# A pre-norm decoder layer on one core: self-attention's side work cut into smaller pieces, cross-attention's bulk loads issued behind the queries' store, the first tiles' list computed in pieces

## The chip, the cores and the metric

The kernel runs on one core of one Trainium2 chip. The metric is the device time of the program in microseconds. The engines are TensorE (PE, with its weight loads as PEld), VectorE (DVE), ScalarE (ACT), GpSimd (POOL) and SyncE (SP), which here only issues DMAs.

## What is computed

One decoder layer on x of 16 batch rows of 256 tokens with 256 features, in float32. Cut to what matters:

```python
x = x + self_attn(layernorm(x))     # 16 heads of 16; local windows of 128, and 128 global tokens
x = x + cross_attn(layernorm(x))    # 16 heads over 120 context tokens, masked
x = x + experts(layernorm(x))       # 8 experts, the top 2 of each token

# self_attn: x gets positions; w = windows of 128
local = softmax(w w^T * scale) w
comp = conv1d(x, conv_w, stride 4) + conv_b          # 64 compressed tokens
gt = concat(comp, global_memory)                     # 128 global tokens
glob = softmax(x gt^T * scale) gt
mix = sigmoid(concat(local, glob) @ gate_w + gate_b)
out = (mix * local + (1 - mix) * glob) @ out_w + out_b
```

## The kernel before

The program has two blocks, `self_attention` and `cross_and_experts`. In each, every engine has its own program, written out by hand: each engine executes its instructions in order and waits on semaphores, and nothing else orders the work.

**Self-attention.** The loop `for b in range(NB + 1)` runs over the 16 batch rows ("rows" below). A row has 8 units, and `unit(s)` splits their number into the half of the tokens, the kind (0 local, 1 global) and the half of the heads. For a unit of kind 0 TensorE makes the scores in `m.scores[0]` (`scores`, L529), VectorE takes the maxima (`maxima`, L969), TensorE subtracts them (`subtract_max`, L576), ScalarE takes exponentials (`exponentials`, L822), and TensorE multiplies by the values (`values`, L596). For a unit of kind 1 scores are made once with the queries as stationary operand for the maxima alone (`queries_scores`, L544, in `m.turn`), the maxima are transposed (`turn_max`, L557) and copied below the queries (`copy_max`, L827), and the scores are made again, already shifted, in `m.scores[1]` (`keys_scores`, L566). After every second unit VectorE transposes the output (`turn_out`, L975) and divides it (`divide`, L979 to L985), which counts up `att_read`.

Beside that stands the row's side work, which belongs to other rows: the normalised rows and their transposes for the rows ahead (`normalise` L941, `apply_norm` L952, `turn_w` L489), the context's transposes, keys and values (`turn_c`, `keys_values` L627 and L630) of the next row, the compression by convolution of the next pair of rows (`compress`, L497, in even rows only, with `add_conv_bias` L960 and `turn_g` L513), and the gate and the projection of the row before (`gate` L604, `squash` L835, `mix_row` L993 and L995, `project` L612, `residual` L1002). Gate, compression, projection and several transposes share one PSUM bank, `m.misc`; `keys_values` and one `turn_w` use halves of `m.turn`, which the units of kind 1 use too. The loop's body has four slots of two units each. Per row TensorE's side work stands so: slot 1 `turn_c` and `turn_w` or `turn_g`; slot 2 a second `turn_w` (even rows) and `keys_values`; slot 3 the whole `gate`, and in even rows the whole `compress` at its end; slot 4 `project`.

GpSimd splits the transposed rows into three bfloat16 parts (`split_w`, `split_g`, `split_k`). SyncE stores them and loads them back in stacked form, six DMAs at a time (`stack_w`, `stack_g`, helper line L228), for the next pair of rows: the queries and keys are read by `scores(b, 0)` and the global tokens by `queries_scores(b, 1)` of that pair's first row.

**Cross-attention.** The loop runs over the same 16 rows with 4 units each. Queries of row b+2 are made in row b (`queries` L1491), split on GpSimd (`split_row` L1433 to L1437), stored by SyncE to `q_scr` (`store_q` L1268) and loaded back stacked in the next turn of SyncE's loop (`stack_q`, L1262). In row b SyncE issues: the two halves of `stack_q(b+1)`, `stack_k` (even rows), the stores of x and of the normalised row b-2, `load_mask(b+3)`, `load_w2(b)`, twice some routing loads or stores, `load_v(b+2)`, and last `store_q(b+2)`. Its waits stand in that order too: `store_q` waits for GpSimd's split, and all later DMAs wait behind it. GpSimd also scatters routing entries into a table in HBM (`dispatch`, L1380).

**Experts.** Tokens are sorted into 71 tiles of 128. The first tiles need only rows 0 to 7 and their list is made by VectorE in cross-attention: `early_tiles` (with `tiles_of_experts`) at the end of row 12, `early_sources` (with `name_experts`) at the end of row 13. These are chains of operations on 8 or fewer columns, each of which waits for the one before (`step`). The tiles' outputs are added to HBM rows by accumulating stores from GpSimd (L1420).

## Time and profile before

| | us |
|---|---|
| median of 3 runs | 1221.88 |
| lowest and highest of them | 1214.57 and 1253.28 |
| profiled execution, time | 1203.42 |
| its span, first to last instruction | 1201.5 |
| TensorE busy in it | 1069.2 (89%) |
| VectorE, ScalarE, GpSimd busy | 661.3, 526.4, 553.3 |
| granted TensorE clock, mean | 0.969 |

The profile is of one execution, which is shorter than each of the three timed runs. Busy times of engines overlap; an engine's busy time beside the length of a stretch says how much of that stretch it stood idle. The four stages stand one behind the other: a start of 45 us, self-attention to about 491 us, cross-attention to about 780 us, and the experts to the end. A float32 matmul is recorded as two passes, so 8 products are 16 matmuls. In TensorE's rows a matmul's end includes the time in which its last columns drain, so consecutive groups overlap a little.

### The profile page before, as it was taken

The page shows a single profiled execution, that of the slowest core. Times are in us where ns is not written, and L with a number is a line of the kernel's source. Part 1 is how long each engine was busy: PE and PEld are TensorE (multiplying, and loading weights), DVE is VectorE, ACT ScalarE, POOL GpSimd, SP SyncE. Part 2 cuts the span into 40 slices and gives each one's busy share as a digit, 9 for nine tenths or more (in the row PEclk, how much of TensorE's full clock was granted, in tenths as well). Part 3 has the DMA queues.
Part 4 walks back from the last instruction along what each step waited for, and adds up shares of the span by engine and source line. Part 5 has one row for each costly group of instructions (what it writes and reads, how often), then busy time and mean ns, then how long its engine had stood idle before and what let it go on. Part 6 is the DMA issues. An engine that isn't in the chain of part 4 may idle for free.

```text
span 1201.5 us, 28326 instructions
## 1 busy us (share of the span) xinstructions
PE 1069.2 (89%) x10917; PEld 914.8 (76%) x10917; DVE 661.3 (55%) x1315; ACT 526.4 (44%) x801; POOL 553.3 (46%) x654
## 2 busy tenths in 40 slices
PE   3488898888888887799989998999979999999995
PEld 2377676777777665677767776799979999999994
DVE  1467777787677776778867788632413212122221
ACT  1355555565655554577767776621112111111110
POOL 7554343445444222243446465446654444445442
PEclk9689999999999999899999899999989999999998
DMA  7463726445262612466555664478988888888882
GB/s 203 133 168 86 181 72 152 104 115 150 68 170 64 176 51 82 102 166 181 144 133 133 152 161 135 159 200 222 245 174 232 241 240 234 242 233 252 227 248 33
DMA packets 207731, 194.19 MB, mean 162 GB/s; under 512 B 62746, under 2 KB 164863, under 8 KB 207600
## 3 DMA queue, kind: packets, MB, share of 16 engines
q1 hardware_dynamic: 189408, 170.86, 49.5%
q0 software_dynamic: 15840, 18.77, 9.3%
q10 hardware_dynamic: 2352, 2.75, 0.8%
q8 instruction: 90, 1.47, 0.5%
q14 instruction: 41, 0.34, 0.1%
HBM read 152.25 MB, written 40.08 MB: 160 GB/s over the span
## 4 chain that ended last, share of the span: by engine, by line
PE 40%; DMA 10%; DVE 4%; issue 2%; POOL 1%; ACT 1%; POOLq 0%; SPq 0%; DVEq 0%; ACTq 0%
PE ps_scores L1669 16%; PE ps_out L1687 8%; DMA out<-y,slot_row 7%; PE ps_turn L1538 3%; PE ps_misc L1570 2%; PE ps_out L1550 2%; PE ps_scores L1525 2%; DMA q_stack<-q_scr 2%; DMA q_scr<-qp 2%; PE ps_misc L1491 1%; PE ps_scores L1518 1%; PE ps_turn L1654 1%; PE ps_misc L1558 1%; DVE ps_scores L2153 1%; DVE xa_rowmax L2156 1%
## 5 line engine op out<-in xcount | busy, mean ns | idle before, releaser
L1669 PEld LDWEIGHTS ps_scores<-xgT,w 128*128 128x128 f32 x2272 | 264.1, 192 | 5.5 <-issue 1.1
L1669 PE MATMUL ps_scores<-xgT,w 128*128 128x128 f32 x2272 | 265.9, 275 | 1.2 <-issue 0.7
L1890 ACT ACTIVATE silu<-ps_scores 128x512 f32<-128x512 f32 x71 | 42.4, 597 | 339.3 <-PE ps_scores L1669 339.3
L822 ACT ACTIVATE sa_probs<-ps_scores 128x1024 f32<-128x1024 f32 x128 | 128.2, 1023 | 105.1 <-PE ps_scores L576 70.2
L2125 DVE TENSOR_TENSOR gate<-ps_scores,silu 128x512 f32<-128x512 f32 x71 | 49.1, 691 | 221.7 <-ACT silu L1890 221.6
L1687 PE MATMUL ps_out<-w2s,gate 128*128 x560 | 134.4, 383 | 7.2 <-DVE y L2131 7.2
L1420 POOL DMA_INDIRECT out<-y,out_row x46 | 72.9, 1585 | 123.4 <-DMA out<-y,out_row 93.5
L1687 PEld LDWEIGHTS ps_out<-w2s,gate 128*128 128x128 f32 x560 | 102.0, 192 | 19.3 <-issue 8.0
L969 DVE TENSOR_REDUCE sa_rowmax<-ps_turn 128x8 bf16<-128x1024 f32 x64 | 78.0, 1218 | 24.7 <-PE ps_turn L544 24.5
L969 DVE TENSOR_REDUCE sa_rowmax<-ps_scores 128x8 bf16<-128x1024 f32 x64 | 76.4, 1193 | 17.4 <-PE ps_scores L529 17.2
L341 POOL TENSOR_SCALAR rstd<-mv 128x2 f32<-128x2 f32 x18 | 4.0, 224 | 169.4 <-DVE mv L944 169.3
L1404 POOL DMA_INDIRECT xg<-xn_rows,slot_row x71 | 70.7, 995 | 23.0 <-issue 20.6
L2153 DVE COPY_PREDICATED_SCALAR ps_scores<-taps,masked_score 128x960 f32 x64 | 77.3, 1207 | 3.1 <-PE ps_scores L1518 2.8
L2131 DVE TENSOR_SCALAR y<-ps_out,slot_share 128x256 f32<-128x256 f32 x70 | 33.8, 483 | 77.0 <-DMA out<-y,slot_row 42.3
L1852 ACT ACTIVATE xa_probs<-ps_scores 128x960 f32<-128x960 f32 x64 | 62.4, 974 | 30.9 <-PE ps_scores L1525 30.4
L2156 DVE TENSOR_REDUCE xa_rowmax<-ps_scores 128x8 bf16<-128x960 f32 x64 | 74.1, 1158 | 2.2
L1380 POOL DMA_INDIRECT table<-entry,slot_i x64 | 64.7, 1012 | 17.2 <-issue 17.2
L975 DVE STREAM_TRANSPOSE blocks<-ps_out 128x512 f32<-128x512 f32 x64 | 45.0, 703 | 50.2 <-PE ps_out L596 49.8
L1538 PEld LDWEIGHTS ps_turn<-ident,xa_probs 128*120 128x120 f32 x512 | 61.9, 141 | 11.8 <-issue 1.5
L1538 PE MATMUL ps_turn<-ident,xa_probs 128*120 128x128 f32 x512 | 68.6, 278 | 0.0
L1420 POOL DMA_INDIRECT out<-y,slot_row x25 | 40.7, 1627 | 58.9 <-DVE y L2131 42.7
L1860 ACT COPY xa_probsT<-ps_turn 120x1024 f32<-120x1024 f32 x64 | 64.8, 1013 | 4.2 <-PE ps_turn L1538 4.2
(260 smaller groups left out, 2081.6 us busy)
## 6 DMA issues: line engine op xcount, KB each, us to landing
w<-in_w1T SPq DMA_DIRECT2D x71, 512.0 KB, 4.1
w<-in_w3T SPq DMA_DIRECT2D x71, 512.0 KB, 5.3
q_stack<-q_scr SPq DMA_DIRECT2D x96, 128.0 KB
qs<-w_scr SPq DMA_DIRECT2D x24, 256.0 KB, 3.9
ks<-w_scr SPq DMA_DIRECT2D x24, 256.0 KB, 4.0
k_stack<-k_scr SPq DMA_DIRECT2D x48, 120.0 KB
w_scr<-wp SPq DMA_DIRECT2D x7, 768.0 KB, 3.7
q_scr<-qp SPq DMA_DIRECT2D x14, 384.0 KB, 4.1
```

The lines of the kernel that those rows point to most:

```text
L822: act.activation(probs[s % 2][:], m.scores[s % 2][:], ACT.Exp, scale=SCALE).then_inc(exped, 1)
L969: dve.tensor_reduce(place, m.turn[:] if kind else m.scores[0][:], AX_X, ALU.max)\
L1380: pool.indirect_dma_start(m.table, bass.IndirectOffsetOnAxis(ap=slot_i[:, t, j:j + 1], axis=0), entry[:, t, j, :], None).then_inc(dispatch ...
L1404: pool.indirect_dma_start(xg[r % 4][:], None, rows, bass.IndirectOffsetOnAxis(ap=slot_row[:, r:r + 1], axis=0)).then_inc(tile_in[r % 4], 16)
L1420: pool.indirect_dma_start(target, bass.IndirectOffsetOnAxis(ap=rows, axis=0), y[r % 2][:], None, compute_op=ALU.add).then_inc(y_added, 16)
L1538: mm = pe.transpose(m.turn[0:KX, h, :], probs[s % 2][:, h, 0:KX], m.ident[:])
L1669: mm = pe.matmul(h_ps[r % 2][:, j, c, :], w13[r % 3][:, j, k, c * P:(c + 1) * P], xgT[r % 2][:, k, :], start=(k == 0), stop=(k == DT - 1))
L1687: mm = pe.matmul(y_ps(r).unsqueeze(1), gate[r % 2][:, k, :], w2s[:, bass.ds(expert * HT + k, 1), :], start=(k == 0), stop=(k == HT - 1))
L1852: act.activation(probs[s % 2][:, :, 0:KX], m.scores[s % 2][:, :, 0:KX], ACT.Exp, scale=SCALE)\
L1860: act.copy(probsT[s % 2][0:KX, :, :], m.turn[0:KX, :, :]).then_inc(turn_read, 1)
L2153: dve.copy_predicated(sc, zero[b % 2][:, n, :].unsqueeze(1).broadcast_to((P, HU, KX)), masked_score[:].unsqueeze(2).broadcast_to((P, HU, K ...
L2156: dve.tensor_reduce(rowmax[s % 2][:], sc, AX_X, ALU.max).then_inc(maxed, 1)
```

## The change

In self-attention:

- `gate(b)` becomes `gate(b, o)`, one half of the output features each. `gate(b-1, 0)` stands in slot 2 ahead of `values(b, 1)`, `gate(b-1, 1)` in slot 3 where the whole gate stood. Within a half the chunks of the first half of heads come first and wait for all but the last `att_read` only. The second half waits for the first half's `tanh`.
- `squash(b, o)` likewise: the first half behind `exponentials(b, 2)`, the second where both stood.
- `compress(p)` becomes `compress(p, k)`, half the taps each, the first where the whole stood (end of slot 3), the second behind `subtract_max(b, 6)` in slot 4.
- `keys_values(b+1)` and its two copies stay in slot 2 in even rows; in odd rows they go to slot 3, and the first split part (`first_k`) with them.
- On ScalarE the first parts (`first_w`, `first_g`, `first_q`) go behind the next exponentials or copies.
- On VectorE `turn_out(b-1, 1, 1)` comes before `normalise(b+3)`; `mix_row(b-1)` before `maxima(b, 7)`, with `divide(b, 0, 1)` behind it; `add_conv_bias` behind `turn_out(b, 1, 0)`.

In cross-attention SyncE's `store_q(b+2)` is issued before `load_mask(b+3)`, `load_w2(b)`, the routing DMAs and `load_v(b+2)`. The first tiles' list is computed in four places: `tiles_of_experts` at the end of row 11, its running sum and what is taken at the end of row 12, `early_sources` in the middle of row 13, `name_experts` at the end of row 13. The late tiles' computation stays the same. The diff, cut to its core:

```diff
-        def gate(b):
-            pe.wait_ge(att_read, OPR * b + OPR)
-            for o in range(DT):
-                for c in range(2 * DT):
-                    mm = pe.matmul(m.misc[:, o * S:(o + 1) * S], gate_w[:, c, o * P:(o + 1) * P], attT[b % 2][:, c, :],
-                                   start=(c == 0), stop=(c == 2 * DT - 1))
+        def gate(b, o):
+            for i, c in enumerate((0, 2, 1, 3)):
+                pe.wait_ge(att_read, OPR * b + OPR - (i < 2))
+                mm = pe.matmul(m.misc[:, o * S:(o + 1) * S], gate_w[:, c, o * P:(o + 1) * P], attT[b % 2][:, c, :],
+                               start=(i == 0), stop=(i == 2 * DT - 1))
             mm.then_inc(gate_made, 1)
...
                 queries_scores(b, 3)
                 subtract_max(b, 2)
+            if old:
...
+                gate(b - 1, 0)
+            if some:
                 values(b, 1)
...
-            if more:
+            if more and even:
                 keys_values(b + 1, side[0])
...
                 queries_scores(b, 5)
                 subtract_max(b, 4)
             if old:
+                pe.wait_ge(tanh_done, DT * (b - 1) + 1)
+                gate(b - 1, 1)
...
                 scores(b, 6)
                 turn_max(b, 5)
+                if more and not even:
+                    keys_values(b + 1, side[0])
                 values(b, 4)
                 keys_scores(b, 5)
...
-                    compress(p + 1)
+                    compress(p + 1, 0)
...
                 queries_scores(b, 7)
                 subtract_max(b, 6)
+                if nxt and even:
+                    compress(p + 1, 1)
                 values(b, 5)
...
             if some:
                 maxima(b, 1)
+            if old:
+                turn_out(b - 1, 1, 1)
             if ahead:
                 normalise(b + 3)
-            if old:
-                turn_out(b - 1, 1, 1)
...
                 maxima(b, 6)
+            if old:
+                mix_row(b - 1)
+            if some:
+                maxima(b, 7)
                 divide(b, 0, 1)
-            if old:
-                mix_row(b - 1)
+                turn_out(b, 1, 0)
             if nxt and even:
                 add_conv_bias(b // R + 1)
...
+            if b < NB - 2:
+                store_q(b + 2)
             if b < NB - 3:
                 load_mask(b + 3)
             load_w2(b)
...
             if b < NB - 2:
                 load_v(b + 2)
-                store_q(b + 2)
...
+            if b == R_EARLY + 5:
+                early_sources()
...
+            if b == R_EARLY + 3:
+                step(dve.tensor_scalar(lane[:], spare[:], -float(SPARE), None, ALU.add))
+                tiles_of_experts(True)
             if b == R_EARLY + 4:
                 early_tiles()
             if b == R_EARLY + 5:
-                early_sources()
+                name_experts(0, N_EARLY, taken_cum)
```

## Rows read from the trace of the kernel before

**Rows 1.** Stages: stretch, length, busy by engine (instructions), clock, DMA share, GB/s.

```profile
45.00:491.00 446.00, 383.56 (x4951) 307.64 (x4952) 325.80 (x533) 247.82 (x334) 176.78 (x226) 0.97 0.45 117
491.00:780.00 289.00, 270.57 (x2860) 213.25 (x2859) 223.69 (x509) 203.96 (x305) 140.18 (x220) 0.97 0.57 150
```

**Rows 2.** The same view of an even, an odd and a longer odd row.

```profile
314.49:343.12 28.63, 25.78 (x326) 21.28 (x324) 21.26 (x35) 16.21 (x22) 13.79 (x16) 1.00 0.29 81
343.12:367.94 24.82, 21.44 (x303) 16.85 (x301) 19.42 (x34) 14.79 (x20) 9.64 (x13) 1.00 0.60 150
127.08:153.37 26.29, 23.00 (x301) 18.04 (x301) 19.43 (x34) 14.88 (x21) 9.64 (x13) 0.94 0.61 157
```

**Rows 3.** Timeline of TensorE, even row: start, length, instructions, [idle before <- releaser].

```profile
317.87 0.65 PE L596 MATMUL ps_out<-sa_probs,vl 128*32 128x128 f32 x16 [0.52 <-DVE blocks L975]
...
320.18 0.64 PE L596 MATMUL ps_out<-sa_probs,vg 128*32 128x128 f32 x16 [0.22 <-ACT sa_probs L822]
...
326.10 3.67 PE L604 MATMUL ps_misc<-attT,gate_w 128*128 128x256 f32 x16
...
332.51 4.06 PE L497 MATMUL ps_misc<-taps,wT 128*128 128x256 f32 x16
...
338.67 0.61 PE L529 MATMUL ps_scores<-qs,ks 96*128 96x128 bf16 x8 [0.63 <-DMA q_stack<-w_scr]
...
340.43 0.62 PE L566 MATMUL ps_scores<-qs,gs 104*128 104x128 bf16 x8 [0.52 <-ACT qs L827]
```

**Rows 4.** Timeline of TensorE, the odd row behind it.

```profile
346.49 0.65 PE L596 MATMUL ps_out<-sa_probs,vl 128*32 128x128 f32 x16 [0.74 <-DVE blocks L975]
...
363.89 0.26 PE L557 MATMUL ps_scores<-neg_ident,sa_rowmax 128*104 128x128 bf16 x1 [0.43 <-DVE sa_rowmax L969]
...
367.49 0.61 PE L544 MATMUL ps_turn<-gs,q_stack 96*128 96x128 bf16 x8
```

**Rows 5.** Timeline of VectorE, the same even row.

```profile
315.98 0.74 DVE L941 BATCH_NORM_STATS2 stats<-xres 128x6 f32<-128x256 f32 x2
...
316.93 0.68 DVE L975 STREAM_TRANSPOSE blocks<-ps_out 128x512 f32<-128x512 f32 x1
...
330.41 0.72 DVE L975 STREAM_TRANSPOSE blocks<-ps_out 128x512 f32<-128x512 f32 x1 [3.34 <-PE ps_out L596]
```

**Rows 6.** Timeline of SyncE's DMA issues, odd row: g's store and stack.

```profile
354.13 0.38 SPq L258 DMA_DIRECT2D g_scr<-gp  x1
357.27 4.48 SPq L228 DMA_DIRECT2D gs<-g_scr  x6
```

**Rows 7.** Stretches of cross-attention: an ordinary row, two long ones, row 13.

```profile
589.80:607.00 17.20, 17.02 (x190) 13.54 (x189) 15.04 (x42) 13.20 (x20) 10.88 (x16) 1.00 0.71 128
607.00:629.60 22.60, 18.55 (x182) 14.72 (x181) 14.09 (x29) 13.29 (x20) 10.68 (x16) 0.92 0.56 146
647.00:669.30 22.30, 19.38 (x181) 15.09 (x180) 13.95 (x28) 13.24 (x20) 10.54 (x16) 0.85 0.48 124
721.80:742.20 20.40, 18.23 (x183) 14.27 (x182) 15.34 (x40) 12.54 (x19) 9.23 (x13) 0.92 0.46 127
```

**Rows 8.** Chain of waits, first long row: start, length, what.

```profile
601.37 9.57 DMA q_scr<-qp
```

**Rows 9.** Timeline of SyncE's DMA issues ahead of that store.

```profile
586.55 4.58 SPq L1262 DMA_DIRECT2D q_stack<-q_scr  x6
...
600.21 0.47 SPq L1289 DMA_DIRECT2D vx<-v_scr  x1
```

**Rows 10.** Timeline of VectorE, the first tiles' list: first and last of 15 operations.

```profile
721.60 0.12 DVE L2039 TENSOR_SCALAR lane<-spare_sb 128x1 f32<-128x1 f32 x1
...
723.72 0.16 DVE L2043 TENSOR_TENSOR taken<-taken_cum 128x7 f32<-128x7 f32 x1
```

**Rows 11.** Timeline of TensorE behind it, and at the end of the first long row.

```profile
622.72 0.96 PE L1518 MATMUL ps_scores<-k_stack,q_stack 96*128 96x120 bf16 x8 [3.87 <-issue]
...
724.68 0.86 PE L1499 MATMUL ps_misc<-ident,xn 128*128 128x128 f32 x4 [2.07 <-DVE xatt L2165]
```

More of the change, by code:

```diff
@@ L688, in tensor_program @@
                 subtract_max(b, 2)
-                values(b, 1)
-            if some:
-                scores(b, 4)
-                turn_max(b, 3)
-            if (nxt or last) and even:
-                turn_w(b + 3, side[1])
-            if more:
-                keys_values(b + 1, side[0])
-            if some:
-                values(b, 2)
-                keys_scores(b, 3)
-            if some:
-                if more:
-                    pe.wait_ge(k_read, b + 2)
-                    pe.wait_ge(v_read, b + 2)
-                if (nxt or last) and even:
-                    pe.wait_ge(wT_read, b + 4)
-                queries_scores(b, 5)
-                subtract_max(b, 4)
             if old:
@@ L718, in tensor_program @@
                     pe.wait_ge(proj_read, b - 1)
-                gate(b - 1)
+                gate(b - 1, 0)
+            if some:
+                values(b, 1)
+            if some:
+                scores(b, 4)
+                turn_max(b, 3)
+            if (nxt or last) and even:
+                turn_w(b + 3, side[1])
+            if more and even:
+                keys_values(b + 1, side[0])
+            if some:
+                values(b, 2)
+                keys_scores(b, 3)
+            if some:
+                if more and even:
+                    pe.wait_ge(k_read, b + 2)
+                    pe.wait_ge(v_read, b + 2)
+                if (nxt or last) and even:
+                    pe.wait_ge(wT_read, b + 4)
+                queries_scores(b, 5)
+                subtract_max(b, 4)
+            if old:
+                pe.wait_ge(tanh_done, DT * (b - 1) + 1)
+                gate(b - 1, 1)
             if some:
@@ L893, in scalar_program @@
                 copy_wT(b + 3, side[1])
-            if b + 1 < NB:
+            if more and even:
                 copy_keys_values(b + 1, side[0])
@@ L897, in scalar_program @@
                 exponentials(b, 3)
-            if b + 1 < NB:
-                first_k(b + 1)
+            if nxt and even:
+                first_w(b + 3)
             if some:
                 exponentials(b, 4)
-            if nxt and even:
-                first_w(b + 3)
+            if more and even:
+                first_k(b + 1)
             if old:
-                squash(b - 1)
+                squash(b - 1, 1)
             if some:
                 copy_max(b, 5)
+                if more and not even:
+                    copy_keys_values(b + 1, side[0])
                 exponentials(b, 5)
@@ L916, in scalar_program @@
                 exponentials(b, 6)
+            if more and not even:
+                first_k(b + 1)
             if some:
@@ L1043, in vector_program @@
                 maxima(b, 6)
-                divide(b, 0, 1)
             if old:
                 mix_row(b - 1)
+            if some:
+                maxima(b, 7)
+                divide(b, 0, 1)
+                turn_out(b, 1, 0)
             if nxt and even:
                 add_conv_bias(b // R + 1)
-            if some:
-                maxima(b, 7)
-                turn_out(b, 1, 0)
             if more:
```

58 lines of the change are left out of this document (34 added, 24 removed).

## The prediction

> **What bounds the kernel now.** I read the stages first, then one steady pair of rows on each engine, then cross-attention's long rows with the chain that ends there. In self-attention (446 us) TensorE is busy 384, in cross-attention (289 us) 271, and no other engine comes near that in either [rows 1]; of the experts the change alters only when their first list is made. So only TensorE's idle time can be won: 62 us in self-attention, 18 in cross-attention.
>
> A steady even row lasts 28.63 us with TensorE busy 25.78, an odd one 24.82 with 21.44, at the full clock [rows 2]. The idle time is thus 2.85 and 3.38 us, 6.2 per pair, and it lies in light slots: a wait for the output's transpose (0.52), for an exponential (0.22), for the maxima's copies (0.52), and in the next row's last slot for maxima (0.43) [rows 3, 4]. The heavy slots are the opposite. The gate's 16 passes take 3.67 us and the compression's 16 take 4.06 in one piece [rows 3], and VectorE then stands idle for 3.34 us [rows 5]. TensorE executes in order, so what counts is whether side work stands ahead of an instruction that would wait anyway. No edit takes side work away; all of them lay it over waits.
>
> **The change, slot by slot.** I lay the durations of the steady rows out in the new order. A slot here goes from one subtraction of maxima of kind 0 to the next.
>
> *Transpose ahead of the statistics.* `turn_out(b-1, 1, 1)` stands behind `normalise` on VectorE: it starts at 316.93 and ends at 317.61, and `values(b, 0)` starts at 317.87 [rows 3, 5]. The statistics ahead of it take 0.95 us (315.98 to 316.93) [rows 5], so it would be done at about 316.7. The values then start at 317.35, when the row's transposes on TensorE end. Late next is the copy of the maxima for `keys_scores(b, 1)`, done at about 317.94 and thus 0.1 us short. Of 0.52 I count 0.44; in the odd row the same copy leaves 0.44 of 0.74 [rows 4]. `normalise` ends as before, so GpSimd gets its variance no later than VectorE needs it back.
>
> *Gate halves.* A half is 3.67/2, about 1.8 us. The first now stands ahead of `values(b, 1)` and `scores(b, 4)`, which wait for exponentials (0.22 and a like one of 0.27). These waits vanish: -0.49 in an even row. The new wait for `att_read` is for `divide(b-1, 1, 1)`, which VectorE ends at about 319.82 [rows 5]; the half begins at about 319.35 and its chunks 1 and 3 are due 0.9 us later, so 0.4 us is spare. Behind it on TensorE would stand `values(b, 1)`, `scores(b, 4)` and VectorE's next maxima. The second half waits for the first tanh, which has some 4 us for it: nothing. Between the halves ScalarE has `squash` in front of `copy_max(b, 3)`, but `turn_max` comes later still.
>
> *Even slots 3 and 4.* Slot 3 keeps one gate half and one half of the compression (2.0 us). Its waits for the transpose and the maxima's copy were 0.46 together and are left uncovered, since both stand behind the gate and ahead of the compression: +0.1, because VectorE is less far ahead. Slot 4 gets the other compression half ahead of `values(b, 5)`. That covers the wait of 0.63 at `scores(b+1, 0)`, which the trace puts down to a DMA but which ends 0.06 us after an exponential [rows 3]. I keep a wait of 0.6 for the turned output and the maxima's copy together, against 0.52: -0.55 in the slot. `add_conv_bias`, now behind `turn_out(b, 1, 0)` on VectorE, is due at `project`; two groups on TensorE (1.0 us) cover its 0.42.
>
> Even row: 0.44 + 0.49 - 0.1 + 0.55 = 1.4 us.
>
> *Odd row.* The keys and values (1.9 us) leave slot 2 for slot 3. In slot 2 the gate half covers 0.50 but `values(b, 2)` and `keys_scores(b, 3)` now wait 0.67 for the transpose and a maxima's copy: +0.17. In slot 3 the keys and values cover 0.46. In slot 4 the mix no longer stands ahead of the last maxima on VectorE (wait 0.43 [rows 4]), but a new one appears, for `turn_out(b, 1, 0)`, as the division and the last maxima (2.3 us) stand ahead of it; the slot's four waits, 1.37 together, become some 0.9, and I count half of that gain. With the first slot's 0.44: 0.44 - 0.17 + 0.46 + 0.25 = 1.0, and 0.2 for the shorter instruction tails that a covered wait also hides: 1.2 us.
>
> Rows 1 to 15 have the gate: 7 even ones x 1.4 and 8 odd ones x 1.2 give 19.4 us. After the last row the gate's first chunks run while the last output is divided, +0.4. Two odd rows, one of them from 127.08, take 26.29 us instead of 24.82 at a granted clock of 0.94 [rows 2]; part of each runs at half clock (1.2 GHz) behind idle time. I count one of them: 1.5. Self-attention: -21 us, with 0 and -44 (7 x 6.2) as its ends.
>
> *The queue of stacked copies.* Splitting of g is tied to VectorE and GpSimd from the odd row's start, so its stack lands about as long after it as before; the last six copies are issued from 357.27 on over 4.5 us and the last landed at 363.6 (361.2 plus 2.4), and their reader `queries_scores(b+2, 1)` starts at 367.49 [rows 4, 6]. The row shrinks by 1.2, the store ahead shifts by nothing: 2 us are left, no cost. The odd row's keys are split some 7 us later; behind their store on SyncE stand the context, the next x and the next w stack, the first of which waits for a split 17 us on. No cost.
>
> *Cross-attention's queue.* An ordinary row takes 17.2 us with TensorE busy 17.0; two take 22.6 and 22.3, at a granted clock of 0.92 and 0.85 [rows 7]. The chain shows why: `store_q` takes 9.57 us, since mask, w2 and v (0.6 MB) were issued just ahead of it (v at 600.21), and two rounds of stacking follow it [rows 8, 9]. The stall on TensorE is 3.87 us [rows 11], 2.74 in the second. With the store first it lands at about 608.3 instead of 610.94, as the mask, issued at the head of the three, landed at about 607 and q carries three times its bytes. But the bulk is now ahead of the stacks: it drains at about 609.9, where the first stack packets would otherwise follow the store by 1.2 us. Gain: 2.2 us a row, and where the stall falls near zero the half clock behind it goes too (6.8 us at half speed in the second row, up to 2.6 us). 2.2 + 2.2 + 1 (half clock, partly) + 0.5 (a third stall of 0.85) = 5.9. Ends: 0, if the stacks are held back by all that the store wins, and 11 (5.4 + 5.1 + 0.8), if both rows become ordinary. In ordinary rows the bulk now meets the stacks; those issued from 586.55 on [rows 9] are through by about 595 and are read at about 602, so 2 to 3 us more costs nothing.
>
> The Trainium skill (DMA: Bandwidth & Descriptors, Queues, rings and completion order) has each DMA engine consume a ring's descriptors in order. This speaks against the edit: the same bytes stand ahead of the first stack in either order. By it alone the gain would be the store's completion time only; the landings in issue order agree.
>
> *First tiles' list.* The small operations from 721.60 to 723.88 hold VectorE for 2.3 us and TensorE for 2.07 [rows 10, 11], and the row is 3.2 longer, at 0.92 of the clock [rows 7]. Cut in 1.0 (row 11) and 1.3 (row 12) each piece still shows nearly whole, since ordinary rows have about 0.25 us of slack: 1.8 against 3.2. The two pieces of row 13 (0.8 and 0.9 us) now stand apart, which I count at 0.5. Gain 1.9; ends 0 and 4.
>
> **Sum.** 21 + 6 + 2 = 29 us off the profiled execution (1203.42 us, span 1201.5): 1174. That execution is 1.5% faster than the median of the runs, 1221.88 (1214.57 to 1253.28), so I scale the gain by 1.015: 1221.9 - 29.4 = 1192.
>
> **Rivals.**
> 1. *The pieces open as many waits as they cover.* In slots 1 and 2 VectorE hardly pauses, and moving TensorE's work cannot hurry it; if they stay tied to it and the new wait of slot 4 is whole, a row gains 0.5, 8 us in all; with 4 in cross-attention 1222 - 12 = 1210. VectorE is busy 21.26 of 28.63 us [rows 2], and its idle time lies in slots 3 and 4 [rows 5]. For it: slots 1 and 2. Against: the 3.34 us of slot 3 are there to be used.
> 2. *The store's new place does nothing*, the bulk holding the stacks back (the page's order of a ring, as this kernel would show it): 1192 + 6 = 1198.
> 3. *Slower.* The g stack becomes late. Its place is `queries_scores(b+2, 1)`, every second row; store and stack take 9.5 us (354.1 to 363.6), so if a transfer held back on SyncE pushed it by one such round, each pair would wait 9.5 - 2 = 7.5 us against 2.6 gained: 7 x 4.9 = 34, less 8 elsewhere: 1248. It turns the sign from 3 + 2 us late on. Against: 2 us of slack and nothing new ahead of it on SyncE.
> 4. *The rows reach TensorE's work*, idle down to a third: -40 - 10: 1171.
>
> **Chances.** Forecast 0.52, rival 4 0.08, rival 1 0.24, rival 2 0.09, rival 3 0.03, and 0.04 for a median like the longest run of before (1253.28), from the expert tiles' DMA waits, untouched by the change. About 2% (24 us) is what a measurement of this kernel can tell from no change: faster 0.60, same 0.33, slower 0.07. Range 1171 (rival 4) to 1216 (rival 1 and half the runs' spread), 0.8; the forecast's own 1180 to 1200.
>
> **What would show it.** Right: an even row of about 27.2 us and an odd one of 23.6; `values(b, 0)` without a wait; no VectorE gap near 3.3 us; the `store_q` that took 9.57 landing in under 7, and rows 7 and 9 (the two long ones) at 20 or less; row 13 under 20. Wrong: a TensorE wait at the gate's second chunks or at `values(b, 6)` over 1 us, `gs<-g_scr` ending waits at L544, or odd rows still above 24.5.

## The result, and the profile after

| | us |
|---|---|
| changed kernel, median of 4 runs | 1173.76 (1169.01 to 1177.01) |
| kernel before, median of 4 runs | 1218.22 (1207.77 to 1253.28) |
| ratio, with its 95% interval | 0.9675 (0.9624 to 0.9725) |
| profiled execution after, time and span | 1169.01 and 1167.2 |
| profiled execution before, time and span | 1203.42 and 1201.5 |
| granted TensorE clock, mean, after and before | 0.976 and 0.969 |

The change is faster by 3.2% by the ratio. The medians lie 44 us apart; the new one is inside the predicted range (1171 to 1216), but near its lower end and 18 us below the predicted 1192. The ratios in this document leave out runs in the chip's occasional slow state, here the one of 1253.28 us, without which the kernel before has a median of 1214.57 and the gain is 41 us. Between the two profiled executions it is 34 us. I cut both traces by ScalarE's exponentials (first of self-attention, first of cross-attention, then the experts' first activation): self-attention went from 447.5 to 419.9 us, cross-attention from 291.8 to 280.3, and the experts from 417.9 to 423.2; the start of 44 us became 0.6 us shorter.

The windows view of the changed kernel has the two stages, then a steady even and a steady odd row (columns as in [rows 1]). They answer [rows 1, 2].

```profile
43.72:463.61 419.89, 379.15 (x4956) 302.81 (x4955) 323.98 (x535) 248.75 (x334) 178.36 (x226) 0.98 0.48 125
463.61:743.92 280.31, 268.39 (x2890) 212.47 (x2889) 223.14 (x509) 204.79 (x304) 142.78 (x223) 0.99 0.60 154
294.72:321.53 26.81, 25.60 (x323) 21.05 (x323) 20.37 (x35) 16.26 (x23) 13.85 (x16) 1.00 0.38 103
271.50:294.72 23.22, 20.98 (x301) 16.62 (x301) 19.88 (x34) 14.78 (x20) 9.83 (x13) 1.00 0.63 157
```

TensorE's work in a row is what it was (25.60 against 25.78, 20.98 against 21.44). Its idle time fell from 2.85 to 1.21 us in the even row and from 3.38 to 2.24 in the odd one. What is left of it stands in TensorE's timeline: an even row, the odd one behind it, and the start of the next even row. It answers [rows 3, 4]; the line numbers have moved, L597 is the old L596, L605 the old L604, L530 the old L529 and L545 the old L544.

```profile
306.12 1.95 PE L605 MATMUL ps_misc<-attT,gate_w 128*128 128x256 f32 x8
...
309.48 0.64 PE L597 MATMUL ps_out<-sa_probs,vl 128*32 128x128 f32 x16 [0.23 <-DVE blocks L999]
...
310.80 2.19 PE L497 MATMUL ps_misc<-taps,wT 128*128 128x256 f32 x8
...
313.72 2.19 PE L497 MATMUL ps_misc<-taps,wT 128*128 128x256 f32 x8
...
339.50 0.61 PE L530 MATMUL ps_scores<-q_stack,k_stack 96*128 96x128 bf16 x8 [0.36 <-ACT sa_probs L837]
...
340.84 0.64 PE L597 MATMUL ps_out<-sa_probs,vl 128*32 128x128 f32 x16 [0.68 <-DVE blocks L999]
...
344.64 0.61 PE L545 MATMUL ps_turn<-gs,q_stack 96*128 96x128 bf16 x8 [0.82 <-DMA gs<-g_scr]
```

Gate and compression stand in halves of about 2 us. In the even row all five waits left are 0.22 or 0.23 us long; the odd row has four such and three longer ones, of 0.30, 0.36 and 0.68 us. The last, at 340.84, is that of unit 6's values for the output's transpose. It stands in every odd row up to 13 (0.91 us in row 14, 1.44 in row 15): the wait that the prediction feared in slot 4. At 344.64 g's stack is late by 0.82 us, in row 11 only.

VectorE's timeline shows the transpose in front of the statistics in an odd row, and that the 3.34 us of idle time in slot 3 [rows 5] became 1.61, now the longest in such a pair of rows:

```profile
272.41 0.72 DVE L999 STREAM_TRANSPOSE blocks<-ps_out 128x512 f32<-128x512 f32 x1
273.05 0.71 DVE L965 BATCH_NORM_STATS2 stats<-xres 128x6 f32<-128x256 f32 x2
...
308.70 0.72 DVE L999 STREAM_TRANSPOSE blocks<-ps_out 128x512 f32<-128x512 f32 x1 [1.61 <-PE ps_out L597]
```

In cross-attention the windows of rows 7, 8, 9 and 13 answer [rows 7]; 7 and 9 are the two that were long.

```profile
578.25:596.84 18.59, 16.98 (x182) 13.45 (x181) 14.10 (x29) 13.20 (x20) 10.65 (x16) 1.00 0.59 138
596.84:614.05 17.21, 17.04 (x190) 13.57 (x189) 15.00 (x42) 13.20 (x20) 10.66 (x16) 1.00 0.70 159
614.05:631.06 17.01, 16.84 (x182) 13.36 (x181) 14.09 (x29) 13.20 (x20) 10.64 (x16) 1.00 0.65 173
...
683.59:701.91 18.32, 16.86 (x182) 13.31 (x181) 15.03 (x38) 12.42 (x19) 9.15 (x12) 1.00 0.48 132
```

Row 7 went from 22.60 to 18.59, row 9 from 22.49 (its window in [rows 7] is cut 0.2 shorter) to 17.01 and row 13 from 20.40 to 18.32, all at the full clock, where the rows before stood at 0.92, 0.85 and 0.92. SyncE's timeline ahead of row 7's stacks answers [rows 9]; the store is now the first of the four:

```profile
572.57 0.37 SPq L1292 DMA_DIRECT2D q_scr<-qp  x1
573.04 0.48 SPq L1238 DMA_DIRECT2D taps<-in_mask  x1
573.57 0.88 SPq L1250 DMA_DIRECT2D w2s<-in_w2T  x1
574.50 0.82 SPq L1313 DMA_DIRECT2D vx<-v_scr  x1
578.80 2.12 SPq L1286 DMA_DIRECT2D q_stack<-q_scr  x2
```

The store landed at 578.79, 6.2 us after its issue, where it had taken 9.57 [rows 8], and the next instruction on SyncE, the first stack, starts there. The stall on TensorE at the end of row 7 fell from 3.87 us [rows 11] to 1.43:

```profile
591.50 0.58 PE L1544 MATMUL ps_scores<-k_stack,q_stack 96*128 96x120 bf16 x8 [1.43 <-issue]
```

Two rows stand below the full clock that did not before: row 14 of self-attention takes 28.11 us at 0.94 (27.69 at full clock before), row 14 of cross-attention 18.06 at 0.91 (17.75 at full clock before).

### The profile page after: what moved, and what is told of

It reads as the page before. It is cut to its first block, busy times and chain, and to the rows that moved or that the text cites. A ratio compares the mean times of both kernels' runs of the same rounds, so it can differ in the third digit from the quotient of the medians.

```text
span 1167.2 us, 28358 instructions
## 1 busy us (share of the span) xinstructions
PE 1060.0 (91%) x10917; PEld 906.4 (78%) x10917; DVE 657.9 (56%) x1315; ACT 526.6 (45%) x801; POOL 554.2 (47%) x654
## 4 chain that ended last, share of the span: by engine, by line
PE 44%; DMA 8%; DVE 4%; issue 2%; ACT 1%; POOL 1%; POOLq 0%; DVEq 0%; ACTq 0%
PE ps_scores L1695 16%; PE ps_out L1713 8%; DMA out<-y,slot_row 8%; PE ps_turn L1564 4%; PE ps_misc L1596 3%; PE ps_scores L1551 2%; PE ps_out L1576 2%; PE ps_misc L1517 2%; PE ps_misc L1584 1%; PE ps_scores L1544 1%; PE ps_turn L1680 1%; PE ps_scores L1625 1%; PE ps_misc L1590 1%; DVE ps_scores L2180 1%; DVE xa_rowmax L2183 1%
## 5 line engine op out<-in xcount | busy, mean ns | idle before, releaser
L1713 PE MATMUL ps_out<-w2s,gate 128*128 x560 | 136.0, 387 | 10.3 <-DVE y L2158 10.3
L1713 PEld LDWEIGHTS ps_out<-w2s,gate 128*128 128x128 f32 x560 | 102.6, 193 | 23.1 <-issue 11.5
L993 DVE TENSOR_REDUCE sa_rowmax<-ps_turn 128x8 bf16<-128x1024 f32 x64 | 77.8, 1216 | 42.1 <-PE ps_turn L545 42.1
L2158 DVE TENSOR_SCALAR y<-ps_out,slot_share 128x256 f32<-128x256 f32 x70 | 33.8, 483 | 84.1 <-DMA out<-y,slot_row 51.5
L605 PE MATMUL ps_misc<-attT,gate_w 128*128 128x256 f32 x256 | 62.6, 387 | 1.5 <-DVE attT L1009 0.7
```

The lines of the kernel that those rows point to most:

```text
L605: mm = pe.matmul(m.misc[:, o * S:(o + 1) * S], gate_w[:, c, o * P:(o + 1) * P], attT[b % 2][:, c, :], start=(i == 0), stop=(i == 2 * DT - 1))
L993: dve.tensor_reduce(place, m.turn[:] if kind else m.scores[0][:], AX_X, ALU.max)\
L1713: mm = pe.matmul(y_ps(r).unsqueeze(1), gate[r % 2][:, k, :], w2s[:, bass.ds(expert * HT + k, 1), :], start=(k == 0), stop=(k == HT - 1))
```

## The experiments

Twelve kernels ran, in four groups; those of a group ran on one chip, and a time is compared inside its group where not said otherwise. Rows are compared across groups: they are told by their length from exponential to exponential: where no DMA and no half clock interferes, it repeats from execution to execution to 0.05 us.

### Each half alone

`sa_only` is the changed kernel with the old cross-attention; `xa_only` is the kernel before with the new one:

```diff
 # sa_only, against the changed kernel
-            if b < NB - 2:
-                store_q(b + 2)
             if b < NB - 3:
                 load_mask(b + 3)
...
                 load_v(b + 2)
+                store_q(b + 2)
...
-            tiles_of_experts(False)
-            ends = running_sum()
+            ends = tiles_of_experts(False)
...
-                name_experts(0, N_EARLY, taken_cum)
+                early_sources()
```

> Only self-attention's part of the change, on the kernel before. If the gains of the parts add up and belong to their stages, self-attention (first exponential to cross-attention's first) falls from 447.5 us to about 420 and cross-attention stays at about 292 with its two long rows of 22.5 us; ratio to before 0.977. Rival: the cross-attention gain of the full change came partly from self-attention's new end state (queues and clock); then cross-attention falls below 287 here.

> Only the store ahead of the bulk loads and the list in pieces, on the kernel before. If the parts add up: self-attention 447 us as before, cross-attention 292 to about 280, ratio 0.990. The expert stage (first tile to the end, 418 us before and 423 after) shows whether its 5 us more belong to this part: near 418 says no, near 423 says that the earlier first tiles meet the DMA queue at a worse moment.

The times were 1184.59 us for `sa_only`, ratio 0.9684 (0.9603 to 0.9764), and 1203.28 for `xa_only`, ratio 0.9843 (0.9793 to 0.9893), against 1221.22 for the kernel before. In the profiles `sa_only` has the changed kernel's self-attention (417.7 us, rows of 26.81 and 23.23) and the old cross-attention (293.6 us, rows 7, 9 and 11 long); `xa_only` has it the other way round (446.6 and 282.9). So the gains of the stages belong to their halves and do not depend on each other, and self-attention's is the larger by far. The timed ratios are too coarse to add up: 0.9684 times 0.9843 is 0.953, below the interval of the whole change (0.9624 to 0.9725), and each half's ratio lies below what I had expected (0.977 and 0.990). Nor did the experts answer my question. They took 431.3 us in `xa_only` and 434.7 in `sa_only`, which has nothing of the edit that I had suspected.

In `xa_only` the new order does not remove all of the long rows: row 7 took 18.13 us and row 9 took 20.99 at 0.92 of the clock, with stalls of 0.97 and 2.22 us.

### The store alone, the list alone

```diff
 # store_only, against the kernel before
+            if b < NB - 2:
+                store_q(b + 2)
             if b < NB - 3:
                 load_mask(b + 3)
...
                 load_v(b + 2)
-                store_q(b + 2)
 # tiles_only, against the kernel before
-            full = tiles_of_experts(True)
+            full = running_sum()
...
+            if b == R_EARLY + 3:
+                step(dve.tensor_scalar(lane[:], spare[:], -float(SPARE), None, ALU.add))
+                tiles_of_experts(True)
```

> Only store_q ahead of mask, w2 and v. By my estimate the two long rows (22.6 and 22.5 us) fall to about 20 each, by what the changed kernel shows to 18.6 and 17.0; row 13 stays at 20.4. If the ring's order made the store's gain void, the rows stay above 22. Queries' stores that took 9.6 and 8.5 us should take 5 to 6.5.

> Only the first tiles' list in pieces. Row 13 falls from 20.4 us to about 18.3, row 12 rises from 17.2 to about 18.3, row 11 does not change by more than 1 and row 14 by more than 0.5: cross-attention 1 to 2 us shorter in all, and the two long rows stay at 22.5. If the pieces were hidden, rows 12 and 13 would both be near 17.3 and 4 us would be won.

Both kernels ran once: 1204.08 us with the store alone and 1207.31 with the list alone, against 1221.22 for the kernel before. With the store alone cross-attention takes 281.4 us, 10.4 less than before. The windows of its rows 7, 9, 11 and 13:

```profile
609.11:626.13 17.02, 16.84 (x182) 13.37 (x181) 14.09 (x29) 13.19 (x21) 10.65 (x16) 1.00 0.55 154
643.34:660.65 17.31, 16.98 (x182) 13.45 (x181) 14.08 (x29) 13.19 (x21) 10.65 (x16) 1.00 0.59 157
677.86:695.04 17.18, 16.98 (x182) 13.45 (x181) 14.08 (x29) 13.19 (x21) 10.65 (x16) 1.00 0.57 133
712.26:732.88 20.62, 18.38 (x182) 14.41 (x181) 15.22 (x40) 12.62 (x18) 9.22 (x12) 0.92 0.45 122
```

The three rows that the store had made long are ordinary and at the full clock, and row 13, which the list makes long, stays. The issues show where the time came from:

```profile
603.42 0.37 SPq L1268 DMA_DIRECT2D q_scr<-qp  x1
603.89 0.48 SPq L1214 DMA_DIRECT2D taps<-in_mask  x1
604.42 0.81 SPq L1226 DMA_DIRECT2D w2s<-in_w2T  x1
605.27 0.54 SPq L1289 DMA_DIRECT2D vx<-v_scr  x1
609.86 4.48 SPq L1262 DMA_DIRECT2D q_stack<-q_scr  x6
```

The store lands 6.4 us after its issue instead of 9.57. The second round of stacks could be issued 2.5 us after that landing (at 612.38, from the landings and issues of the same stretch), where before it took 3.58 (614.53 less 610.95). The bulk, issued ahead of the stacks, had landed by 611.4, 1.5 us after the first of them was issued, and no delay from it shows here.

Other rows are less clear. Behind the stores of rows 6, 8 and 10 the second round came 2.6 to 4.7 us after the first in the four profiles with the old order (both of before, `sa_only`, `tiles_only`) and 2.5 to 4.5 us in three with the new one (after, `xa_only`, `store_only`), so neither order stands out. The stores themselves took 5.2 to 9.6 us and 3.5 to 6.4. One issue of a stack took 1.50 us in the changed kernel and one 2.22 in `xa_only`, where most take 0.6; whether the bulk is the cause no run tells. The gain of 10.4 us is thus one pair of profiles. With 1.8 us taken off for the list it is 9.7 in the changed kernel and 7.1 in `xa_only`, against the first profile of before.

With the list alone rows 12 to 14 take 53.5 us instead of 55.4, a gain of 1.8, and rows 7 and 9 stay long (20.9 and 21.4). But row 11 took 22.97 us at 0.85 of the clock, where I had allowed it 1 us over its 18.0, and so the stage as a whole was no shorter (291.9 us). TensorE stalls for 3.20 us there ahead of the scores that read the stacked queries, as it does for 3.27 in row 11 of `sa_only`, which has the old list, and not at all in `xa_only`, which has the new one; so that stall goes with the old place of the store and not with the list. In the changed kernel rows 12 to 14 take 54.7 us, 0.7 less than before, as row 14 is at 0.91 of the clock there. The waits of 0.81 and 1.03 us that the pieces of rows 11 and 12 open at the transposes of x stand in both this kernel and the changed one.

### Undoing one piece of self-attention

All four are the changed kernel with one piece undone. Each ran once, and the changed kernel did not run beside them, so it is the rows that are compared. In steady rows (26.81 and 23.23 us with everything in place):

| | undone | even row | odd row |
|---|---|---|---|
| `gate_whole` | one gate in slot 3 | 28.18 (+1.37) | 24.44 (+1.21) |
| `conv_whole` | one compression at slot 3's end | 27.51 (+0.70) | 23.23 (0) |
| `kv_early` | odd rows' keys and values in slot 2 | 26.80 (0) | 23.71 (+0.48) |
| `norm_first` | transpose behind the statistics | 27.25 (+0.44) | 23.67 (+0.44) |

```diff
 # gate_whole
-                gate(b - 1, 0)
...
-                pe.wait_ge(tanh_done, DT * (b - 1) + 1)
-                gate(b - 1, 1)
+                gate(b - 1)
 # conv_whole
-                    compress(p + 1, 0)
+                    for k in range(DT):
+                        compress(p + 1, k)
...
-                if nxt and even:
-                    compress(p + 1, 1)
 # kv_early
-            if more and even:
+            if more:
...
-                if more and not even:
-                    keys_values(b + 1, side[0])
 # norm_first
-            if old:
-                turn_out(b - 1, 1, 1)
             if ahead:
                 normalise(b + 3)
+            if old:
+                turn_out(b - 1, 1, 1)
```

> The changed kernel with gate and squash in one piece in slot 3 again. The changed kernel's steady rows are 26.81 us (even) and 23.23 (odd). If the first half covers two waits for exponentials in slot 2, as the prediction has it (0.5 us by the records, up to 0.7 from start to start), both rows grow by 0.5 to 0.7 us and VectorE's idle time before a transpose in slot 3 goes back above 3 us. If the spread over slots matters more than these two waits, they grow by over 1 us.

> The changed kernel with the compression in one piece at the end of slot 3. Odd rows keep 23.23 us. Even rows grow from 26.81 by 0.5 to 0.7 if the second half covers the wait for the exponential in slot 4 (0.63 before); by less than 0.2 if mix_row's new place had already removed that wait.

> The changed kernel with the odd rows' keys and values in slot 2 again. The prediction had this edit at +0.46 - 0.17: odd rows then grow from 23.23 by 0.3 us, even rows keep 26.81. Rival: it is worth nothing or costs, since it moves the same 1.9 us from two uncovered waits to two others; then odd rows are at 23.2 or below.

> The changed kernel with normalise ahead of turn_out(b-1, 1, 1) again. The prediction has 0.44 us in each row, so 27.25 and 23.67. If the gate half behind it takes up the delay, since TensorE would wait for maxima there anyway, the rows grow by less than 0.2.

`norm_first` came out to the hundredth, `conv_whole` at the upper end of what I had expected and `kv_early` at 0.48 instead of 0.3. The gate is worth twice what I had put on it: the second case of my expectation, over 1 us. TensorE's timeline of `gate_whole` in slots 1 and 2 of an even row, all its waits there:

```profile
253.91 0.62 PE L530 MATMUL ps_scores<-q_stack,k_stack 96*128 96x128 bf16 x8 [0.23 <-ACT sa_probs L834]
...
257.42 0.64 PE L597 MATMUL ps_out<-sa_probs,vg 128*32 128x128 f32 x16 [0.22 <-ACT sa_probs L834]
258.85 0.62 PE L530 MATMUL ps_scores<-q_stack,k_stack 96*128 96x128 bf16 x8 [0.79 <-ACT sa_probs L834]
```

Of 1.37 us, 1.01 are the last two waits (0.22 + 0.79), neither of which the changed kernel has. The other 0.36 are no wait: the later slots have the same waits in both kernels, and TensorE is recorded as busy for that much longer with the same work. The second had been 0.27 in the kernel before. As I read it, moving the transpose ahead lets TensorE reach these scores sooner while the exponential ends where it did: the wait grew by what another edit had won (0.27 + 0.44 = 0.71 of 0.79; in the odd row 0.28 before and 0.68 here), and only the gate half in front covers it. No kernel undid both, so this is argued, not shown. The prices also do not add: 0.44 + 1.37 + 0.70 = 2.51 us in the even row against 1.81 for the change as a whole.

### The wait that the change opened

`divide_first` takes the last maxima of a row from in front of the division and puts them behind it. The transpose of unit 6's output, for which TensorE waits, stays behind both; it is not moved ahead of the maxima, as the expectation has it:

```diff
+                divide(b, 0, 1)
                 maxima(b, 7)
-                divide(b, 0, 1)

                 turn_out(b, 1, 0)
```

> The changed kernel, only that in slot 4 VectorE divides the first half's output and transposes it ahead of the last maxima, not behind. In the profile after, TensorE waits 0.68 us in odd rows at the values of unit 6 for the output's transpose, which is what the prediction named as the price of the odd row's slot 4. Theory: that wait goes and nothing else becomes late, so odd rows shrink from 23.23 to 22.6 to 22.8 us, even rows stay within 0.1 of 26.81, and self-attention gives 4 to 5 us. Rival: the last maxima become late instead (they feed the subtraction and the exponential of unit 7), and the wait moves there: odd rows 23.2 or longer, even rows longer by up to 0.4, self-attention equal or up to 4 us longer.

Odd rows shrink by 0.16 us only, to 23.07, and even rows stay at 26.81. VectorE had stood idle for 0.81 us before the last maxima. The division now fills this, the maxima start 0.2 us later and the transpose 0.9 us earlier. The wait of 0.68 is gone from TensorE's timeline, but another stands one group later:

```profile
242.87 0.62 PE L567 MATMUL ps_scores<-qs,gs 104*128 104x128 bf16 x8 [0.52 <-ACT qs L842]
```

That is the shifted scores' maxima, copied by ScalarE. 0.68 - 0.52 = 0.16: the rival's account, but at a small gain, not a loss. A transpose ahead of the maxima was not tried. The kernel's time was 1191.67 us and its ratio 0.976 (0.9655 to 0.9866); the changed kernel beside it had 0.9738 (0.9608 to 0.9867), so the timing tells nothing between them. No version beat the changed kernel.

### The bulk out of the way

`bulk_last` issues mask, w2, routing and v behind the next turn's stacks:

```diff
+            if b > 0:
+                bulk(b - 1)
...
-            if b < NB - 3:
-                load_mask(b + 3)
-            load_w2(b)
...
-            if b < NB - 2:
-                load_v(b + 2)
```

> The changed kernel, only that in cross-attention mask, w2, routing and v of a row are issued behind the next turn's two halves of stacked queries, so that nothing stands in the queues between the store of the queries and their stacks. If the bulk ahead of the stacks held them back (my theory for the bound on the gain, 1.2 us of drain per row in which the stall shows), the stalls left at the long rows go: rows 7 and 14 from 18.6 and 18.1 to about 17.2, cross-attention 280 down to 277 to 278. Rival: order in the queue matters only for the store itself, whose completion was the wait, and cross-attention stays within 1 us of 280; the stacked keys or the stores of x behind the bulk could even come later and cost 1 to 2 us.

The time was 1196.67 us, ratio 0.9757 (0.9632 to 0.9882). Cross-attention took 307.6 us, beside 299.4 in the changed kernel and 301.8 in `divide_first`, which has the same order there, on the same chip. No long row became shorter, and row 11 grew to 22.4 (17.7 and 19.0 in the two beside it). GpSimd's timeline shows what is new in that row:

```profile
668.41 0.83 POOL L1457 TENSOR_SCALAR taps<-taps 128x240 int32<-128x240 int32 x1 [3.90 <-DMA taps<-in_mask]
```

GpSimd, which prepares the masks and splits the queries in its own order, now waits for the mask, in rows 9, 10 and 11 for 7.25 us together, and never does so in the other two. The edit moved the other loads too, so the mask's share of the 6 to 8 us is argued. My expectation of 2 to 3 us gained failed. It doesn't settle by itself whether stacks without bulk in front would be faster, since the late mask covers that.

### The same two kernels again

> The changed kernel itself, as the base of the two runs beside it and to see how far its cross-attention and its experts differ from execution to execution. If the long cross-attention rows of the second group of experiments (18.4 to 18.6 us from row 6 on instead of 17.2) belong to the chip or the execution, they can show here too; if they come from the edits of those four kernels, the changed kernel never shows them. Self-attention is expected at 419.9 us with rows of 26.8 and 23.2, time 1169 to 1185.

> The kernel before itself, profiled a second time, to see whether its cross-attention also differs between profiled executions. In the profiles of seven kernels built on the changed one, TensorE's completions at the values (unit 3) reach ScalarE 0.5 to 1.9 us late in every row from row 6 on, where GpSimd's scatters into the table begin, and cross-attention takes 297 to 308 us; in the first profiles of before and of the changed kernel and in the four of the first group of experiments no completion is late by 0.3 us more than twice. Theory: the lateness belongs to the chip and not to the edits. Then, on a chip where it occurs, before shows it too, its ordinary rows from row 6 on take 18.4 to 18.7 and 17.7 us instead of 17.2, and its cross-attention 300 to 312 us instead of 291.8; on a chip where it does not occur, its rows stay as they were and nothing is told apart. Rival: the changed kernel's order brings the completions and the scatters together, and before shows none of it on any chip.

The changed kernel's median here was 1203.70 us (1182.03 to 1217.07) beside 1223.62 for the kernel before, ratio 0.9738 (from two of its four runs). I had expected 1169 to 1185. Its cross-attention is like that of the other six profiles of the second and third groups (297 to 308 us). Of its stages self-attention is the known one (417.2 us), but cross-attention takes 299.4 instead of 280.3. The kernel before, profiled again on yet another chip, had 1231.00 us (two runs) and takes 450.3 and 302.9 (447.5 and 291.8 at first). Beside it on that chip the very same kernel had 1218.74 (three runs), a ratio of 1.0101 (1.0039 to 1.0162): the intervals do not hold all of the spread, and a difference of 1% says nothing here. ScalarE's timeline at the same place of row 8, first the changed kernel's first profile:

```profile
602.95 0.59 ACT L1866 COPY qT<-ps_misc 128x512 f32<-128x512 f32 x1 [0.71 <-PE ps_misc L1517]
603.55 0.59 ACT L1894 COPY xa_outT<-ps_out 128x512 f32<-128x512 f32 x1
```

and its second, with TensorE's group that it waits for:

```profile
600.81 0.64 PE L1576 MATMUL ps_out<-xa_probsT,vx 120*32 120x128 f32 x16
600.91 0.59 ACT L1866 COPY qT<-ps_misc 128x512 f32<-128x512 f32 x1 [0.72 <-PE ps_misc L1517]
...
603.38 0.59 ACT L1894 COPY xa_outT<-ps_out 128x512 f32<-128x512 f32 x1 [1.87 <-remote]
```

and the kernel before, second profile:

```profile
640.55 0.58 ACT L1868 COPY xa_outT<-ps_out 128x512 f32<-128x512 f32 x1 [1.74 <-remote]
```

TensorE's group is recorded as ended at 601.45, and it is the same group at the same distance as in the first profile, but the copy that needs it starts 1.9 us later. The semaphore's own event in the trace lies at 603.35. I compared these events with TensorE's recorded ends: in cross-attention over fifty completions are late by 0.3 to 4 us in each of the seven changed kernels of the second and third groups of experiments and in the second profile of before, and at most three in the first profiles of both kernels and in the four of the first group. All eight series start in row 6. So before has it as well; the rival (the new order brings it about) falls.

Cross-attention is 11 us longer with it in the kernel before and 19 in the changed one. About 10 us of each lie in the last row, which takes 33.0 to 33.8 us in the eight profiles with late completions and 23.5 to 24.3 in the six without. GpSimd issues four gathers and at least four scatters back to back there, and ScalarE waits in the changed kernel's second profile:

```profile
741.42 0.97 ACT L1878 ACTIVATE xa_probs<-ps_scores 128x960 f32<-128x960 f32 x1 [6.54 <-remote]
```

TensorE's group is recorded as ended at 734.92, and its event lies at 741.39. Rows 0 to 14 grow by 9.3 us in the changed kernel (256.4 to 265.6) and by 1.0 in the kernel before (268.1 to 269.1); that the stalls of the old order cover a part of it is my reading of this, and was not tried.

## Why the prediction was right, and where its terms were off

**The bound and the direction: right.** Only TensorE's idle time was to be won, and it was won there: of 62 us of idle time in self-attention [rows 1] 41 are left (419.89 less 379.15), of 18 in cross-attention 12 (280.31 less 268.39).

**The rows' order of magnitude: right; both were under-sized.** Predicted were 1.4 and 1.2 us, measured 1.81 (28.62 to 26.81) and 1.59 (24.82 to 23.23).

- *Transpose ahead of the statistics, 0.44 and 0.44*: `norm_first` gives 0.44 and 0.44 back. Right, with the 0.1 by which the maxima's copy stays late.
- *Gate halves, 0.49 less 0.1 in the even row*: 1.37 in `gate_whole`. This is the step that failed most. I priced the two covered waits at what the rows of before show (0.22 and 0.27), not at what they become once another edit brings TensorE there earlier (0.22 and 0.79). In the odd row, where I had put a loss of 0.17 in slot 2 (with the keys and values gone from it), it is 1.21. The prediction kept waits of 0.67 there, and the changed kernel has 0.46.
- *Compression halves, 0.55*: 0.70 in `conv_whole`. Right within 0.15.
- *Keys and values in odd rows, 0.46 less 0.17*: 0.48 in `kv_early` against 0.3.
- *Slot 4 of the odd row, 0.25*: the new wait for `turn_out(b, 1, 0)` is there, 0.68 us in the profile, and the waits of slot 4 went from 1.37 to 1.26 in all, a gain of 0.11. `divide_first`, where the wait is gone, is only 0.16 shorter.

**Half clock: 1.5 predicted, 2.9 measured in rows 3 and 5.** The rows of 26.29 [rows 2] and 26.26 us, both at a granted clock of 0.94, became 23.23: 3.06 and 3.03 less, of which 1.59 each is the row's own gain. I had counted one of two. Against this stands row 14, at 0.94 in both profiles of the changed kernel (28.11 and 28.19 us, where `sa_only` and `bulk_last` have 26.5 at full clock), 1.6 us that the prediction does not have. Five profiles with the old self-attention (before twice, `xa_only`, `store_only`, `tiles_only`) have two to four odd rows of 26.3 to 27.5 us, in different places; of the four with the new one (after twice, `sa_only`, `bulk_last`) none has one, nor has `conv_whole`, while `divide_first` has one, row 1 at 26.62 us and 0.96. `gate_whole` and `kv_early` have three each again: `gate_whole`'s row 11 took 26.10 us at 0.93 and `kv_early`'s 25.33 at 0.93. `norm_first`, with odd rows of 23.67, has none, so a row's length alone does not decide it.

**Self-attention in all: 21 predicted, 27.6 measured.** The rows 0 to 14 give 25.5, the last row and the tail behind it 2.1. Over more profiles it is more: the five with the old self-attention took 446.6 to 452.5 us, the four with the new one 417.2 to 419.9, medians 450.3 and 417.6, a gain of 33.

**The store: 5.9 predicted, 10.4 measured alone.** The mechanism (it need not queue behind the bulk) was right. The term that failed is the loss behind it: I let the bulk, which now stands ahead of the stacks, hold back their first packets and so took 2.2 us a row of a stall of 3.87. In `store_only` the stall disappeared whole, and with it the half clock in its row: 5.59 us in row 7 and 5.18 in row 9 (22.61 to 17.02 and 22.49 to 17.31), and 0.83 in row 11, less what rows 13 and 14 lose again (0.24 and 1.23, row 14 at 0.91 of the clock), and small differences elsewhere: 10.4. In the changed kernel 1.43 us of stall are left in row 7, and in `xa_only` 0.97 and 2.22 in rows 7 and 9. The rule cited from the Trainium skill (DMA: Bandwidth & Descriptors, Queues, rings and completion order) gave the store's completion alone. The landings in `store_only` are in keeping with it (609.84 for the store, then 610.03, 610.77 and 611.41 for mask, w2 and v), but the stack's round behind the store took 2.5 us instead of 3.58, so nothing in this trace shows the stacks waiting for the bulk. Whether they do in the rows where a stall is left stays open.

**The list: 1.9 predicted, 1.8 measured in `tiles_only` and `xa_only`, 0.7 in the changed kernel, whose row 14 lost clock.** Each piece shows nearly whole: 0.81 and 1.03 us of wait for pieces that I had put at 1.0 and 1.3.

**The rivals.** The first (as many new waits as old) falls: one new wait of 0.68 stands against 1.59 + 0.68 us covered in its row. The second (the store's place is void) falls by 10.4 us. The third (g's stack late) did show itself, at L545 in row 11, by 0.82 us and once (and in the second profile once, by 0.40): a steady stack landed 1.2 us before its reader and not 2, as the odd row shrank by more than I had said and store and transfers took 10.3 us (282.12 to 292.43) instead of 9.5. In row 11 they took 11.9 (332.49 to 344.4). The fourth (rows at TensorE's work) gave 1171 and the median is 1173.76, but for another reason: idle time in a pair of rows is 3.45 us, not the 2.1 that it named, and the rest came from elsewhere, clock and store among it. That the median lies within 3 us of it is chance.

**The experts** were to be untouched. They took 417.9 us before and 423.2 after in the profiles, 417.9 and 430.1 in the two profiles of before, and 418 to 450 over all fourteen. This spread, with the half clock's, is larger than the difference between the profiled gain (34 us) and that of the medians (44, or 41 without the run of 1253.28); which stage makes that difference the record does not say. What makes the experts' time vary was not tried.

## What to carry to other kernels

A wait that a trace shows is the price of covering it only if nothing else moves: when one edit brings an in-order engine to the next wait sooner, that wait can grow by as much (0.27 to 0.79 here, argued and not shown), so walk the row with all edits in and price each piece of cover last. A store that others wait for belongs ahead of bulk loads whose readers have a row of time, but not every load that looks like bulk has it: with mask, w2 and v issued one place later GpSimd waited for the mask, and cross-attention was 6 to 8 us longer. Compare stages and row lengths rather than totals, since rows repeated to 0.05 us in kernels whose totals differed by 30.

## What the runs showed of the hardware that I had not expected

- **TensorE's completions can reach the other engines late, by 0.5 to 1.9 us in an ordinary row and by up to 6.5 us in the last, in some executions (those of three of the four groups of experiments) and only in part of the program.** They begin in row 6, the first in which GpSimd scatters into the table, and in steady rows the late groups start at the same two places: their recorded ends lie 1.85 and 6.65 us behind the row's first exponential, where a scatter of 1.07 us that began at 1.81 or 5.67 us still runs. They are worst in the last row, where gathers and scatters follow each other without a pause. The scatters take the same time in the profiles without it (1.06 to 1.07 us). Where no completion was late, the experts' first step is shorter too, 4.96 against 6.42 us in the changed kernel. What differs between these executions stays open: each group ran on another chip and on one occasion, so chip and occasion are not told apart, and a kernel without the scatters was not tried. The Trainium skill (Perfetto Trace Analysis, Tensor Engine Instruction (MATMUL, LD_WEIGHTS)) says that a matmul's reported end is an estimate and its semaphore is updated once PSUM has acknowledged the bytes. This trace agrees that the recorded end is not what releases the others: it and the event lie 0.04 us apart in one execution (603.49 and 603.53) and 1.90 in another (601.45 and 603.35).
- **The same change came out at 3.2% in one measurement and 2.6% in another**, 0.9675 (0.9624 to 0.9725) and 0.9738 (0.9608 to 0.9867), intervals that overlap. Self-attention's part held in every profile (417 to 420 us against 447 to 452), while cross-attention's was 11.5 us in one pair of profiles and 3.5 (302.9 to 299.4, from two chips) in the pair with late completions.
